# A drain carries TensorE's count of finished pairs in the message stage of a graph recommender kernel

## The reference

```python
def _propagate(all_emb, rows, cols, vals):
    acc = all_emb
    x = all_emb
    for _ in range(N_LAYERS):                      # 3
        x = jax.ops.segment_sum(vals[:, None] * x[cols], rows, num_segments=N_NODES)
        acc = acc + x
    return acc / (N_LAYERS + 1)
...
users_emb = all_users[users] + _upsample_nearest(mm_users[users])
items_emb = all_items + _upsample_nearest(mm_items)
rating = users_emb @ items_emb.T
return jax.nn.sigmoid(rating + bias_user[users] + bias_item.T)
```

## Time and profile before

| | us |
|---|---|
| runs: median (lowest to highest) | 6020.74 (6016.39 to 6022.49) |
| profiled execution: span, first to last instruction | 6906.3 |
| VectorE busy | 5194.9 (75%) |
| ScalarE busy | 4083.1 (59%) |
| TensorE products busy | 4000.4 (58%) |
| GpSimd busy | 2327.8 (34%) |

### The profile page before, as it was taken

One profiled execution on the slowest core, in us unless ns is written; L12 is line 12 of the kernel. 1 busy time (PEld: TensorE's weight loads), 2 busy tenths in 40 slices (PEclk: granted clock), 3 DMA queues, 4 the chain that ended last, 5 costly groups with the idle time before them and its releaser, 6 DMA issues.

```text
span 6906.3 us, 175021 instructions
## 1 busy us (share of the span) xinstructions
PE 4000.4 (58%) x57424; PEld 3370.0 (49%) x57662; DVE 5194.9 (75%) x7652; ACT 4083.1 (59%) x10026; POOL 2327.8 (34%) x2074
## 2 busy tenths in 40 slices
PE   5300211056766766776566666677656666657777
PEld 4300111045665665665555555566555565556652
DVE  9999999965555555999655555599965555559997
ACT  0055565244444445999555555599955555559987
POOL 0044333034444444000455555500045555550000
PEclk9755555577777777999777778799978777779998
DMA  9500000044444444665444444466544434446669
GB/s 338 201 0 0 0 0 0 5 112 142 143 142 140 143 138 140 162 161 138 133 144 141 141 141 142 140 162 161 138 136 144 140 140 142 141 136 162 161 166 317
DMA packets 737418, 921.22 MB, mean 133 GB/s; under 512 B 68254, under 2 KB 585279, under 8 KB 736977
## 3 DMA queue, kind: packets, MB, share of 16 engines
q1 hardware_dynamic: 646112, 670.30, 34.5%
q0 software_dynamic: 90944, 249.26, 10.0%
q10 hardware_dynamic: 304, 1.00, 0.1%
HBM read 533.93 MB, written 386.43 MB: 133 GB/s over the span
## 4 chain that ended last, share of the span: by engine, by line
DVE 41%; issue 21%; PE 16%; another core or an unknown queue 13%; ACT 5%; DMA 2%; DVEq 2%; POOL 0%; SPq 0%; POOLq 0%; ACTq 0%
DVE ring L1235 9%; PE psum L1473 6%; DVE store L1028 5%; DVE ring L1192 4%; PE psum L1475 4%; DVE ring L1277 4%; PE psum L1511 3%; ACT ring L671 3%; DVE ring L1271 3%; DVE new L1286 3%; DVE store L1006 2%; DVE total L823 2%; DVE store L1007 2%; DVE ring L1268 1%
## 5 line engine op out<-in xcount | busy, mean ns | idle before, releaser
L737 POOL DMA_INDIRECT posts<-ring x1884 | 1908.0, 1013 | 3078.9 <-ACT ring L657 2614.5
L657 ACT ACTIVATE ring<-ring 128x64 f32<-128x64 f32 x7536 | 1885.0, 335 | 1782.3 <-DVE ring L1192 1109.9
L1473 PE MATMUL psum<-store,ring 128*128 x15072 | 2192.4, 261 | 1007.9 <-DVE ring L1235 584.7
L1473 PEld LDWEIGHTS psum<-store,ring 128*128 128x128 bf16 x15072 | 1801.7, 124 | 1175.8 <-issue 1148.7
L1192 DVE TENSOR_REDUCE ring<-psum 128x512 f32<-128x1024 f32 x942 | 1151.1, 1222 | 1513.7 <-remote 1468.5
L1475 PE MATMUL psum<-store,ring 128*128 x15072 | 2104.8, 229 | 150.2 <-issue 148.3
L1475 PEld LDWEIGHTS psum<-store,ring 128*128 128x128 bf16 x15072 | 1626.8, 115 | 226.4 <-issue 183.4
L1235 DVE TENSOR_SCALAR ring<-ring,lane_f 128x1024 bf16<-128x1024 bf16 x1884 | 843.3, 489 | 10.6 <-DMA ring<-lanes_d 10.6
L1505 PE MATMUL psum<-ring 128*128 128x64 bf16 x7584 | 562.4, 198 | 232.3 <-DVE ring L1271 228.5
L720 POOL TENSOR_TENSOR ring<-store 128x1024 f32<-128x1024 f32 x157 | 370.6, 2361 | 800.8 <-DVE store L1007 363.5
L1511 PE MATMUL psum<-ring 128*128 128x64 bf16 x15168 | 528.9, 194 | 151.9 <-DVE ring L1277 150.2
(11 more groups left out here) (232 smaller groups left out, 3970.6 us busy)
## 6 DMA issues: line engine op xcount, KB each, us to landing
ring<-lanes_d SPq DMA_DIRECT2D x471, 512.0 KB
ring<-posts SPq DMA_DIRECT2D x240, 516.0 KB
store<-posts SPq DMA_DIRECT2D x234, 516.0 KB
out<-new SPq DMA_DIRECT2D x96, 500.0 KB, 8.5
posts<-store SPq DMA_DIRECT2D x2, 20640.0 KB, 115.8
posts<-store SPq DMA_DIRECT2D x2, 20124.0 KB, 88.6
posts<-ring POOLq DMA_INDIRECT x1884
ring<-runs_d SPq DMA_DIRECT2D x78, 256.0 KB
```

Of the source, the lines that this page charges most:

```text
L657: last = nc.scalar.activation(of, of, ACT.Copy, scale=vring[:, h, c * BLOCK + b:c * BLOCK + b + 1])
L737: pool.indirect_dma_start(out=posts[:, :], out_offset=bass.IndirectOffsetOnAxis(ap=dring[:, h, c:c + 1], axis=0), in_=msg[:, n, :], in_off ...
L1473: pe.matmul(psum[:, c, b * 2 * F:(b + 1) * 2 * F], of, xflat[:, bass.ds(at_d[c] * F + k * XT, 2 * F)], start=(k == 0), stop=False, skip_gr ...
```

## The change

No other instruction is added or moved, and the other engines' programs are the same. The program holds 38 such drains in its loops and behind them; they are executed 942 times.

```diff
                                 pe.matmul(psum[:, c, b * 2 * F:(b + 1) * 2 * F], of, xflat[:, bass.ds(at_d[c] * F + k * XT, 2 * F)],
                                           start=(k == 0), stop=False, skip_group_check=True)
-                                last = pe.matmul(psum[:, c, (2 * b + 1) * F:(2 * b + 2) * F], of, xflat[:, bass.ds(at_d[c] * F + (k * XT + 2 * F), F)],
-                                                 start=False, stop=(k == 1), skip_group_check=True)
+                                pe.matmul(psum[:, c, (2 * b + 1) * F:(2 * b + 2) * F], of, xflat[:, bass.ds(at_d[c] * F + (k * XT + 2 * F), F)],
+                                          start=False, stop=(k == 1), skip_group_check=True)
                         if n % 2 == 1:
-                            last.then_inc(s_sent, 1)
+                            pe.drain().then_inc(s_sent, 1)
```

## The result

The change takes 6114.19 us (6106.71 to 6115.27), the kernel before 6021.61 (6016.39 to 6027.63), in four runs each: a ratio of 1.0151 [1.0139, 1.0163], 93 us slower. The forecast was 6178, 157 us slower; the result also lies just under the 100 to 250 us that the prediction named as the sign of being right.

The account below looks back on a forecast made before the run. The prediction saw TensorE and VectorE close to balance in the first halves of the layers. It added 131 us for borders and 26 us for the later count, 157 in all, to 6020.74: 6178 us, range 5900 to 6420.

Parts of the forecast that it names:

- the sign of being right: Runs slower by 100 to 250 us, while in the profile the join's wait may shrink and no border runs on after 0.08 us.
- the main case: Whole kernel: the drain holds TensorE back, 157 us slower, 6178 us, within 6040 to 6420; chance 0.58.
- The profiled execution isn't the one that is timed: First halves: the profile's 886 us above the runs is waiting for late counts, mostly from recording; 683 us idle remain.
- The faster rival: Joins: the product's late count is in the runs too and the drain's is not; 5850 us, chance 0.25.
- The 683 us are TensorE's own time at the lower clock: First halves: VectorE's remaining idle time, 0.73 us a pair, comes from 32 products taking about 2.6 us at 1.2 GHz.
- The product loses its count: Last product of each pair: it keeps its place and length, so the cost is 0.
- The drain ends 0.1 us late: End of each pair: the count leaves 0.1 us later than from a product; 26 us, on 527 pairs at half.
- A border without a wait costs 0.63 us: TensorE between pairs: gap of 0.58 us in place of 0.08, plus 0.13 for wider steps of the first four products.
- Only then come the register addition (0.032) and the wait (0.051): Behind each drain: only these two sequencer steps of the next pair, in us, precede the way to its first product.
- 415 borders: TensorE's borders without a wait, 78 behind look-ups excluded: 415 pay 0.63 us each, 261 us of TensorE's time.
- Half of TensorE's delay reaches the end: Joins: a share between 0.68 and 0.44 of TensorE's delay counts, taken as one half: 131 us of 261.
- the rival "no difference": Every pair: hots, scatters and joins set the pace and hide the drain; 6021 us within 12, chance 0.12.

Follow-up runs that it names:

- e0: The kernel before, unchanged, run and recorded again: 6026.94 us, ratio 1.0001; the recording spans 6021.9 us.
- e5: The kernel before without GpSimd's scatters to main memory, GpSimd raising the counts of their landing itself: 5571.51 us.
- e3: Against the kernel before, the count stays on the last product and a drain without a count follows it: 6114.49 us, ratio 1.0140.
- e7: The change with the register loads for the next two pairs and the first load of a look-up issued ahead of the drain: 6048.76 us, ratio 1.0030.
- e4: The change with a second drain, without a count, behind each first one: 6153.96 us, ratio 1.0217.
- e10: The kernel before, no drain, first layer's register loads moved ahead, one at the end of each pair behind its last product: 5907.50 us, ratio 0.9804.
- e8: The kernel before, no drain, first layer's register loads moved ahead, two among the products of the pair before a look-up: 6010.56 us, ratio 0.9969.

## Why the prediction was right, and where it was not

Its sign was right, and the bounds of the main case, 6040 to 6420, hold the result; the 157 us were too many for 93. That they came so near was luck in part, as the steps show:

- **The profiled execution isn't the one that is timed: right.** The 683 us of VectorE's idle time that I left to the runs are 665 in the recording of e0 (busy 758 of 1043, 665 of 861 and 667 of 851 us). That recording as such holds counts back, for which I called in the Trainium skill ("NOTIFIC — the notification-queue block", section 7.1), is not borne out: no later recording shows it. The faster rival wanted 0.33 us of lateness a pair; there was 0.09 at most.
- **The 683 us are TensorE's own time at the lower clock: right in part, in the first layer.** In the recording of e0 the granted clock is 0.82, 0.88 and 0.88 for the 0.72 to 0.76 of the earlier trace rows, and a pair's products take 2.16, 1.95 and 1.96 us on average, not 2.6; VectorE works 2.41, 2.12 and 2.12 us a pair. In the first layer the look-ups come on top of TensorE's time. In the other two VectorE's idle time goes with the scatters: it falls from 196 to 11 us in the second when they are left out (e5).
- **The product loses its count: nothing.** e3 agrees.
- **The drain ends 0.1 us late: mis-sized.** It ends 0.02 us behind the product, and the count 0.01 later. The term of 26 us is nothing.
- **A border without a wait costs 0.63 us: right for the plain border, by a sum whose parts were off.** A gap of -0.19 us became 0.42, 0.61 in all, where the prediction had 0.50 for the gap. This is far above the 0.18 that the Trainium skill's "TensorE: Matmul & The Clock Gate", section Single matmul latency, gives, issue included, for a product that stands alone; here the measurement decides. The other 0.13, the wider steps of the first four products, are there (the fourth starts 0.37 us behind the first in place of 0.25, medians), but the whole pair got no longer: 2.18 us on average for 2.28.
- **"Only then come the register addition (0.032) and the wait (0.051)": the step that failed.** At every second border and ahead of each look-up the load of line 1445 stands there too, 0.34 us with 0.05 and more beside it. e7 puts 65 us on that one omission.
- **415 borders: wrong.** 233 ran on, 116 of them in the first layer. I had excluded the 78 behind a look-up as having no such border; they pay most, (346 - 291) / 78 = 0.70 us each. In the first layer 79, 78 and 78 borders lose, 152 / 235 = 0.65 us each.
- **Half of TensorE's delay reaches the end: wrong in each layer, near the mark as a mean.** In the first layer the borders that pay lost 152 us and the half 103: two thirds arrive, and the rest is hidden mainly where TensorE waited for the hots anyway (40 us). In the other two nothing arrives. "GpSimd with 636 of 1163 has room" came from the disturbed recording: undisturbed it is busy 633 us of 861 in the second layer, and of the rest 172 us are the 0.30 us and more ahead of each scatter and 47 are waits for ScalarE. My own floor of 2474 us for three halves, 825 each, already stood close to what the later two take; I compared it with the mean of three, 2751 / 3 = 917, and so missed that the rival "no difference" holds in two layers of three.

The total thus came out near by luck, because two errors offset: too many paying borders in layers where the scatters hide them, and loads left out where nothing hides them.

## What to carry to other kernels

A drain on an empty engine costs little by itself (e4); what it costs is the work that the sequencer did ahead under the running engine, so list every register load, address and wait that stands behind it, and ask of each stage separately whether another engine's pace hides it. The same list shows what to gain without a drain: loads that already stand on an idle engine, moved one by one to where the sequencer has a lead, were worth 117 us here (e10). Where a profiled execution is far longer than its runs, have the same kernel recorded again before reading its waits.

## What the runs showed of the hardware

- The lead of TensorE's sequencer is about 0.8 us (the drain's median length). One load of four registers, 0.34 us, mostly fits into it (borders with a load: 0.24 us on average in the kernel before, recorded again, 0.87 in the change); two in one pair made that pair 0.6 us longer (e8: 2.39 us against 1.80).
- A drain ends 0.02 us behind the last product; a second one behind it lengthens the gap by 0.05 to 0.08 us (e4).
- Shorter idle stretches around the look-ups went with a higher granted clock over the first layer, 0.82 to 0.88, and with a first pair behind each look-up that was 0.46 us shorter (e10). In the timeline of the change the pair behind a look-up runs at the level of 1.2 GHz (granted clock 0.50 from 1505 to 1507 us), two products in 0.16 us, where the pair ahead of the look-up, at the higher level (1.00 from 1499.5 to 1501), takes 0.09:

```profile
1500.05 0.22 PE L1473 MATMUL psum<-store,ring 128*128 x1
...
1500.14 0.22 PE L1473 MATMUL psum<-store,ring 128*128 x1
...
1505.09 0.29 PE L1473 MATMUL psum<-store,ring 128*128 x1
...
1505.25 0.29 PE L1473 MATMUL psum<-store,ring 128*128 x1
```
